# A second FFN with its inner units on partitions: weights stationary, token blocks of two, two and four tiles

## What is computed

```python
x = x + 0.5 * ffn(layernorm(x), A, B, Wr)
x = x + attn(layernorm(x), wq, wkv, wo)
x = x + 0.5 * ffn(layernorm(x), A, B, Wr)

def ffn(x, A, B, Wr):               # 64 experts of rank 16, 16 taken for each token
    scores = x @ Wr.T                                  # [tokens, 64]
    top_vals, top_idx = top_k(scores, 16)
    G = scatter(softmax(top_vals))                     # [tokens, 64], zero where not taken
    h = einsum('nd,krd->nkr', x, A)                    # [tokens, 64 * 16]
    return 2.0 * einsum('nkr,kdr->nd', h * G[:, :, None], B)
```

## Time and profile before

| | |
|---|---|
| median of three runs | 1035.66 us (1035.02 to 1035.69) |
| the profiled execution | 1035.98 us |
| its span, first to last instruction | 1033.9 us |
| granted TensorE clock, mean | 0.998 |
| TensorE busy | 1025.1 us (99%) |
| VectorE, ScalarE, GpSimd busy | 687.0, 554.5, 534.2 us |
| chain that ended last | PE 92%, DVE 4%, ACT 2%, DMA 1%, issue 1% |
| HBM read, written | 102.37 MB, 63.44 MB |

### The profile page before, as it was taken

The page is one execution under the profiler, slowest core; times in us unless marked ns, Lnnn a source line. Parts: engine busy times, 40 slices in busy tenths (PEclk is TensorE's granted clock), DMA queues, the critical chain, the costliest instruction groups (busy, mean ns, idle before and its releaser), DMA issues.

```text
span 1033.9 us, 18709 instructions
## 1 busy us (share of the span) xinstructions
PE 1025.1 (99%) x5588; PEld 889.3 (86%) x5588; DVE 687.0 (66%) x1815; ACT 554.5 (54%) x1480; POOL 534.2 (52%) x473
## 2 busy tenths in 40 slices
PE   8999999999999999999999999999999999999998
PEld 8999888888888888888888888888877788889997
DVE  6778842432477677766766766766777988666553
ACT  4112455554366676676676667676776566531110
POOL 5431378996279777779777779777420000000000
PEclk9999999999999999999999999999999999999999
DMA  9700254772734443443443453443588878840000
GB/s 367 319 0 1 81 210 177 271 265 92 248 93 137 157 144 115 150 162 132 151 147 118 152 162 133 143 149 127 159 286 299 302 240 289 290 156 11 21 20 31
DMA packets 83704, 168.17 MB, mean 163 GB/s; under 512 B 8528, under 2 KB 24912, under 8 KB 82640
## 3 DMA queue, kind: packets, MB, share of 16 engines
q1 hardware_dynamic: 83664, 167.68, 46.8%
HBM read 102.37 MB, written 63.44 MB: 160 GB/s over the span
## 4 chain that ended last, share of the span: by engine, by line
PE 92%; DVE 4%; ACT 2%; DMA 1%; issue 1%; POOL 0%; POOLq 0%
PE bank L276 27%; PE bank L278 27%; PE bank L277 27%; PE bank L565 4%; PE bank L554 3%; PE bank L583 3%; PE bank L332 1%; DMA o_raw<-keep_o 1%; DVE o_lo L970 1%; PE bank L284 1%; DVE prob L1104 1%; ACT o_hi L634 0%; ACT bank L680 0%; DVE ow_lo L970 0%; PE bank L359 0%
## 5 line engine op out<-in xcount | busy, mean ns | idle before, releaser
L1321 POOL TENSOR_SCALAR ve<-mv 128x1 f32<-128x1 f32 x24 | 6.4, 265 | 305.9 <-DVE mv L977 305.6
L680 ACT ACTIVATE bank<-bank,nmax 128x128 f32<-128x128 f32 (+1 forms) x256 | 105.7, 450 | 6.1 <-DVE nmax L1091 6.1
L1104 DVE TENSOR_SCALAR prob<-bank,rinv 128x128 f32<-128x128 f32 (+1 forms) x256 | 95.1, 413 | 4.6
L276 PE MATMUL bank<-xc_lo,wq_hi 128*128 128x512 f32 x224 | 91.8, 410 | 0.0
L1091 DVE CUSTOM_DVE_ANT_0 bank<-bank,mask 128x128 f32<-128x128 f32 (+1 forms) x256 | 83.5, 388 | 11.4 <-PE bank L278 11.4
L276 PE MATMUL bank<-o_lo,ow_hi 128*128 128x512 f32 x224 | 89.1, 398 | 1.0 <-DVE o_lo L970 0.9
L276 PE MATMUL bank<-xc_lo,wk_hi 128*128 128x512 f32 x224 | 88.7, 396 | 0.0
L634 ACT CAST o_hi<-o_raw 128x1024 fp32r<-128x1024 f32 x56 | 59.1, 1056 | 53.8 <-DMA o_raw<-keep_o 47.2
L278 PE MATMUL bank<-xc_hi,wq_hi 128*128 128x512 f32 x224 | 87.9, 392 | 0.0
L278 PE MATMUL bank<-xc_hi,wk_hi 128*128 128x512 f32 x224 | 87.5, 391 | 0.0
L278 PE MATMUL bank<-o_hi,ow_hi 128*128 128x512 f32 x224 | 87.4, 390 | 0.0
(11 more groups left out here) (168 smaller groups left out, 3152.8 us busy)
## 6 DMA issues: line engine op xcount, KB each, us to landing
o_raw<-keep_o SPq DMA_DIRECT2D x49, 512.0 KB, 4.5
keep_v<-out_hl SPq DMA_DIRECT2D x64, 256.0 KB, 2.3
v<-keep_v SPq DMA_DIRECT2D x64, 256.0 KB, 3.5
keep_o<-att_comb SPq DMA_DIRECT2D x60, 256.0 KB, 2.9
keep_o<-att SPq DMA_DIRECT2D x45, 256.0 KB, 3.2
stage_v<-wv SPq DMA_DIRECT2D x4, 2048.0 KB, 9.4
stage_wq<-wqk SPq DMA_DIRECT2D x16, 512.0 KB, 3.3
keep_vraw<-out_raw SPq DMA_DIRECT2D x64, 128.0 KB, 2.1
```

The costliest lines, as they stand in the source:

```text
L276: nc.tensor.matmul(dst, a_hi, b_lo, start=first, stop=False, skip_group_check=onto)
L680: nc.scalar.activation(sp[b][:, a:e], sp[b][:, a:e], ACT.Exp, bias=nmax[:, c:c + 1], scale=-1.0, accum_out=rsum[:, c:c + 1]).then_inc(s["e ...
L1104: nc.vector.tensor_scalar(prob[:, b, a:e], sp[b][:, a:e], rinv[:, c:c + 1], None, ALU.mult).then_inc(s["p_ready"], 1)
```

## The change

1. **Second FFN, products.** The weights are now stationary and the tokens moving. Scores and inner units come out with units on partitions, so the 64 transposes of gated units go. Tokens are handled in three blocks: u = 0 and 1, 2 and 3, 4 to 7 (u counts tiles in the FFN's order; the moving width is 256, 256, 512). Scores are a product of their own for each block, 64 units wide (`pe2_scores`), then eight chunks of 128 inner units (`pe2_up`) into two banks in turn.
2. **Gates.** The scores are copied out and transposed to tokens (`pe2_score_transposes`), routed as before (`dve_top`), the gates are written twice side by side, transposed back (`pe2_gate_transposes`) and copied out (`gate_t`). Each up chunk is copied to SBUF by ScalarE first (`act2_product` into `h_raw`), and multiplied there when the gates have come (`dve2_gated`); then follow the high half (`act2_high`) and low half (`dve2_low`). For that the inner units are stored rank by rank instead of expert by expert, which also changes the host's layout of A and B and the pattern of the gate product in the first FFN (L1059).
3. **Down products** of all eight tiles stand at the end, tile by tile into two banks in turn. The combine of tile 0 stands in VectorE's list behind gate product 4 of the last block, the others behind that block.
4. **Output product.** Transposes of the first two tiles at m = 54 and 55 (before: one tile at 55), the block sum at m = 50 instead of 51, back transposes at 52 instead of 53.
5. **Last pair of heads.** ScalarE converts token groups 1, 3 and 5 ahead of the exponentials instead of behind them.
6. **Head.** The up product of tile 0 takes the matmuls with the weights' high half first, those with the low half later.

```diff
         def pe_ffn_up_first(pe):
...
+            def high(k):
+                for c, (a, b) in enumerate(CHUNKS):
+                    if c < 2 and k == 0:
+                        pe.wait_ge(s["up_hi"], c + 1)
+                    elif c == 0:
+                        pe.wait_ge(s["up_hi"], k + 2)
+                    nc.tensor.matmul(ub[c][:, 0:b - a], xT_lo[:, k, :], upT_hi[:, k, a:b], start=k == 0, stop=False)
+                    nc.tensor.matmul(ub[c][:, 0:b - a], xT_hi[:, k, :], upT_hi[:, k, a:b], start=False, stop=False)
...
+            high(0)
+            high(1)
+            low(0)
+            high(2)
+            low(1)
+            low(2)
+            pe_ffn_transpose(pe, 1)
+            high(3)
+            low(3)
...
+        def pe2_up(pe, b, c):
+            i, n = NR * b + c, P * len(BLOCKS[b])
+            if i >= 2:
+                pe.wait_ge(s["h_copied"], i - 1)
+            else:
+                pe.wait_ge(s["o_sum"], 6)
+            cols = slice(EXPERTS + c * P, EXPERTS + (c + 1) * P)
+            for k in range(KD):
+                last = mm3(hb[i % 2][:, 0:n], upT_hi[:, k, cols], upT_lo[:, k, cols],
+                           xT2_hi[b][:, k, :], xT2_lo[b][:, k, :], k == 0, k == KD - 1)
+            last.then_inc(s["up_ready"], 1)
+
+        def pe2_down(pe, u):
+            b = block_of(u)[0]
+            if u >= 2:
+                pe.wait_ge(s["combined"], NT + u - 1)
+            else:
+                pe.wait_ge(s["xT_split"], 2 * NT)
...
+        def dve_second(dve):
...
+            dve2_route(dve, 0)
+            dve2_route(dve, 1)
+            dve.wait_ge(s["ct_added"], 8)
+            dve2_stats(dve, 4)
+            dve2_stats(dve, 5)
+            dve2_normalise(dve, 4)
+            dve2_normalise(dve, 5)
+            dve2_stats(dve, 6)
+            dve2_stats(dve, 7)
+            dve2_route(dve, 2)
+            dve2_route(dve, 3)
+            dve2_transposed(dve, 4)
+            dve2_transposed(dve, 5)
+            dve2_normalise(dve, 6)
+            dve2_normalise(dve, 7)
...
+            for c in range(NR):
+                dve2_gated(dve, 2, c)
+                if c > 0:
+                    dve2_low(dve, 2, c - 1)
+                if c == 4:
+                    dve2_combine(dve, 0)
+            dve2_low(dve, 2, NR - 1)
+            for u in range(1, NT):
+                dve2_combine(dve, u)
...
             for j in range(4):
                 u = 4 * p + j
                 act_prob_transposed(act, u, j)
+                if final and j < 3:
+                    act_o_tokens(act, 2 * j + 1)
...
-                elif m in (19, 43, 51):
-                    dve_o_sum(dve, {19: 0, 43: 1, 51: 2}[m])
+                elif m in (19, 43, 50):
+                    dve_o_sum(dve, {19: 0, 43: 1, 50: 2}[m])
...
+            pe.wait_ge(s["downagain_loaded"], 16 * 16)
+            pe2_down(pe, 0)
+            pe2_gate_transposes(pe, 2)
+            for u in range(1, NT):
+                pe2_down(pe, u)
```

More of the change, by code:

```diff
@@ L335, in pe_ffn_gated_transpose, with pe_ffn_down @@
                     last.then_inc(s["hT_ready"], 1)
[L337 to L340, removed]
+        def pe_ffn_down(pe, n, dst=fb, first=False):
+            if not first:
                 pe.wait_ge(s["combined"], n)
@@ L346, in pe_ffn_down @@
                     pe.wait_ge(s["hT_split"], 2 * n + 1 + i // 4)
[L347 to L350, removed]
+                last = mm3(dst[:, :], hT_hi[:, i, :], hT_lo[:, i, :],
+                           downT_hi[:, i, :], downT_lo[:, i, :], i == 0, i == NR - 1)
+            last.then_inc(s["down_ready"], 1)
@@ new lines, in build_macaron, with block_of, half_cols, pe2_transpose @@
+        BLOCKS = ((0, 1), (2, 3), (4, 5, 6, 7))
+        def block_of(u):
+            b = min(u // 2, 2)
+            return b, u - BLOCKS[b][0]
+        def half_cols(b):
+            return slice(0, 4 * P) if b == 2 else slice(2 * P * b, 2 * P * (b + 1))
+        def pe2_transpose(pe, u):
+            pe.wait_ge(s["xn_ready"], NT + u + 1)
+            if u >= 2:
+                pe.wait_ge(s["xT_split"], NT + u - 1)
+            for k in range(KD):
+                last = nc.tensor.transpose(tb2[u % 2][:, k * P:(k + 1) * P], xn2[u % 2][:, k * P:(k + 1) * P], ident[:])
+            last.then_inc(s["xT_ready"], 1)
@@ new lines, in pe2_gate_transposes @@
+        def pe2_gate_transposes(pe, b):
+            pe.wait_ge(s["gate_ready"], BLOCKS[b][-1] + 1)
+            if b == 0:
+                pe.wait_ge(s["o_c12"], 2)
+            else:
+                pe.wait_ge(s["gateT_copied"], b)
+            for u in BLOCKS[b]:
+                i = u - BLOCKS[b][0]
+                last = nc.tensor.transpose(gtb[:, i * P:(i + 1) * P],
+                                           gate2[u // 4][:, u % 4, :, :].rearrange("p a e -> p (a e)"), ident[:])
+            last.then_inc(s["gateT_ready"], 1)
@@ L1743, in _ @@
             pool_pair(pool, LAST, final=True)
-            with pool.Fori(0, NT) as t:
-                pool_rstd(pool, t + NT, 0)
+            for j in range(NT, NT + NT // 2):
+                pool_rstd(pool, j, 0)
+                pool_rstd(pool, j, 1)
         @block.tensor
```

348 lines of the change are left out of this document (255 added, 93 removed).

## The result

The changed kernel takes 1032.68 us (median of 8 runs, 1032.31 to 1033.13), the kernel before 1035.23 in the 8 runs beside it: ratio 0.9974 [0.9965, 0.9983], so 2.6 us or 0.26% faster, just over the 0.2% that can be told from no change. The forecast was 1032.7. It was worked out from a base of 1035.66, though, 0.43 us above the 1035.23 measured here: the gain was forecast as 3.0 us and is 2.6.

The account below looks back on a forecast made before the run. The prediction took TensorE's products and its few standstills as the bound. Gains of 1.1 (second FFN), 1.1 (last pair), 0.5 (last block sum) and 0.3 (head) made 3.0 us, forecast 1032.7 us, range 1030.2 to 1035.3.

Follow-up runs that it names:

- The last kernel of the study: The changed kernel with the combines of tiles 0 and 1 moved ahead on VectorE and the last three wo pieces loaded later: 1030.55 us, ratio 0.9947.

## What to carry to other kernels

When an edit makes TensorE's work shorter, look at once for the first instruction that hands a bank back and count what stands ahead of it in its engine's program order: here that one place cost 1.82 of 2.24 us, and moving two instructions made the stretch 1.97 us shorter. Where the chain in order of time leaves TensorE for tens of microseconds, price the round on the other engines and not only TensorE's stalls. Price every stall over a start-to-start price, also those too short to have a row among the waits, and compare two stretches only from the same kind of event to the same kind. A stall behind a transfer that one execution shows is a sample; see it in a second trace before an edit is credited with its end.

## What the runs showed of the chip that was not expected

The granted clock at the start differs from run to run with the same code. In the window from 8.16 to 12.40 us it is 0.60 in the changed kernel; with both combines moved, an edit a thousand microseconds away, the same window reads

```profile
8.16:12.40 4.24, 4.24 (x25) 3.94 (x25) 4.03 (x5) 3.33 (x4) 1.14 (x1) 1.00 1.01 355
```

and with wo later

```profile
8.16:12.40 4.24, 4.24 (x14) 4.24 (x15) 4.08 (x5) 3.42 (x4) 1.11 (x1) 0.50 1.01 371
```

so 14 products' starts against 25 in the same time. The last kernel of the study has a clock of 1.00 in that window, but its starts say otherwise:

```profile
8.16:12.40 4.24, 3.65 (x12) 3.65 (x13) 4.10 (x6) 3.59 (x4) 0.52 (x1) 1.00 1.02 388
```

```profile
9.56 0.52 PE L316 MATMUL bank<-upT_hi,xT_lo 128*128 128x384 f32 x1
9.88 0.52 PE L317 MATMUL bank<-upT_hi,xT_hi 128*128 128x384 f32 x1
```

Products of 384 columns stand 0.32 us apart, the price at the 1.2 GHz level. Why the window reads 1.00 is not shown; at the head of a trace the distance of the starts has to be read beside it.

The first transposes of prob start at 288.87 us in the kernel at full clock, and at 289.57 and 289.55 in the two at half clock. But they start at 288.74 in the changed kernel, whose clock is mixed (0.60), and at 289.36 in the one with the combine of tile 0 first, which is at full clock by its starts (0.17 apart) and has its first up product 0.4 us later than the one at full clock above (8.55 against 8.11). So the clock there is worth 0.7 us at most, and not always that. Small gains are therefore best read from inside a trace, from one start to another, and not from the spans.
